# Centred output weights, the first batch's keys rotated on GpSimd, and new orders of work

## The chip, the cores and the metric

The kernel runs on one core of a Trainium2 chip. The metric is the device time of one launch in microseconds (us). Its engines are TensorE (PE: matrix products), VectorE (DVE), ScalarE (ACT), GpSimd (POOL) and SyncE (SP), whose queue issues the DMAs; each goes through its own instructions in order and waits on semaphores for the others. SBUF is the on-chip memory; PSUM holds the results of TensorE in eight banks.

## The reference, cut to what matters

```python
x = L0_attn_x                                        # (8, 1024, 256) fp32
x = x + layernorm(attn(layernorm(x)))                # 16 heads of 16, rotary, causal
x = x + layernorm(ffn(layernorm(x)))

def attn(x):                                         # qkv, bias, rotary on q and k
    scores = q @ k^T / 4, masked above the diagonal; softmax; @ v
    return out @ proj_w.T + proj_b
def ffn(x):
    return gelu(x @ U1 @ V1 + b1) @ U2 @ V2 + b2     # rank 64, 1024 wide
```

All is fp32. Both inner results go through a layernorm over the last axis (256) before they are added to the residual, so a mean over that axis that is taken out of the output weights and the output bias beforehand changes nothing in the end.

## The kernel before, in words

The work is eight batches of 1024 tokens; a batch has two halves `c` of 512 tokens, and four groups `g` of four heads. Per half: statistics and normalisation of the rows (`ln_*`), transposition (`xt`), products with the weights for queries and keys (`qk`; `p` is 0 for queries, 1 for keys) and values. Queries and keys are rotated (`rope`, three steps, function `rotate`, lines 537 to 553), rounded by ScalarE (`round`), and what the rounding left is computed (`rest`, function `rest_of`, line 555). Both parts are written to DRAM (`send`, line 624) and loaded back into QK in the layout that the scores need: for the first group in four pieces, one for each half and for keys or queries (`load_first`, line 634), for all others with `load_group` (line 649).

Per group TensorE computes all scores twice: `max` (twenty products, each reduced by VectorE, line 1015) for the rows' maxima, which are turned and written into QK as a further row (`shift`), and `score`, whose result ScalarE takes through the exponential (line 1206). GpSimd zeroes the part above the diagonal (`select`), and `product` multiplies with the values. A `max` over the second half of the sequence waits for both second-half pieces of the first load.

Behind the fourth group of a batch the heads' sums are inverted, `att_scale` multiplies, `proj` projects, and VectorE adds the bias (`proj_out`, line 1041). Then follows the layernorm of the result: statistics (`y_stats`, `y_dev`), GpSimd's `y_pow` (variance plus epsilon, minus the mean, power -0.5, their product), ScalarE's `y_rows` (line 1216: one instruction a row of tiles, scale and bias), and GpSimd's `residual` (line 1321). The feed-forward part runs behind the last groups over pieces `i` of 1024 tokens; its last layernorm is `f_spread`, `f_ypow`, `f_norm` (ScalarE, line 1245; two on VectorE in the last piece, line 1128) and `f_res` (GpSimd, line 1351; two on VectorE, line 1135).

The order of each engine's instructions is written out by hand as a string of letters, one for each step (`ORDERS`, line 154), and each of TensorE's results has its bank in a string of digits (`PLACES`, line 229). `taken_by` (line 126) says which engine has a step that could run on two. For batch 0 all of `rope` and `rest` is VectorE's, for the others GpSimd's:

```python
def rope_by(b, c, p):
    return "DVE" if b == 0 else "POOL"
```

Of the kernel before, what the change touches and what calls it, by code (L numbers as in the profile page):

```python
# [73 lines left out]
HALVES = (0, 1), (2, 3)  # L74


def steps_by_name():
# [4 lines left out]
        "ln_stats ln_rows y_stats y_rows": [(b, c, j) for b, c in halves for j in range(4)],  # L82
# [22 lines left out]
        "proj_out residual": [(b, c, q) for b, c in halves for q in (0, 2)],  # L105
        "first_turn first_turn_out first_low first_shift fold_weights fold fold_out f_load f_zero f_fill f_weights f_rest": [()],
# [8 lines left out]
        "f_norm f_res f_store": [(i, js, a) for i in parts for js in HALVES for a in (1, 0)],  # L115
# [5 lines left out]
def rope_by(b, c, p):  # L121

    return "DVE" if b == 0 else "POOL"


def taken_by(engine, step):

    what, *at = step
    if what in ("rope", "rest"):
        return engine == rope_by(*at[:3])  # L130
    if what in ("f_norm", "f_res"):
        last = at[0] == NB - 1 and at[2] == int(what == "f_norm")
        return (engine == "DVE") == last
    return True

# [20 lines left out]
        "HxxqqqqqqqqvvvvxxfqqqqqqqvqvvvxmmxmmmmqvFqqvhhmmqmmmqqmssqmssmqmsmsmvmvmsmxptmsmmsmxmssmpsmpmsssmsspssmsmq"  # L156
        "ssmqmssmmsspmsssmpmssmmsmmpsmmtpsssmssqqmssmpssmqmmssqsmpssmppsssmssqqssmmppmsssmsmsspssmsmpssmsspmsmtssmp"
        "mssmpssmspmssssspsssmpssmsssppmmssspssmspssmsspmssmspmssspmsssmpmssssptmsmsspmssmpmssmpsssmssmspssmspsmsms"
        "spmsssspmsmssppmsssmpssmsmspsmssmpssssmtpsssmmspssmsspmmssppmssvvmmssvvmssssxpsmssxsssmpppmmssqqmssmpssmqq"
        "mssmqqssssmvqvqvvssmmtpjmssmjpjssssmjmsssspmmsspxsssmspxppssssmqqqqmmsspqmssmqssmppsmssmqqssmmpjmssssjsmps"  # L160
# [131 lines left out]
def block_kernel(nc, x, w_qkv, b_qk, b_v, w_proj, b_proj, u1, v1, b1, u2, v2, b2,  # L292
# [27 lines left out]
    with ExitStack() as ctx:  # L320
# [425 lines left out]
        def tensor(e):  # L746
# [11 lines left out]
            for step in ORDER["PE"]:  # L758
# [649 lines left out]
```

## Time and profile before

| what | us |
|---|---|
| median of three runs (lowest, highest) | 1206.66 (1205.65, 1210.28) |
| the profiled execution, its time | 1208.03 |
| its span, first to last instruction | 1206.3 |
| TensorE busy | 1155.2 (96%) |
| VectorE busy | 941.1 (78%) |
| ScalarE busy | 941.8 (78%) |
| GpSimd busy | 658.8 (55%) |

The profile is of one execution. "PE" in it is a matrix product and "PEld" the load of its weights, which overlaps it; the ends of products are modelled, so products that follow closely count as busy throughout. Idle time stands with the engine and line that ended it. The granted clock (PEclk) is that of TensorE as a share of full speed.

### The profile page before, as it was taken

To read this page: it belongs to the slowest core of one execution; us is meant where nothing else is said; L and a number is where in the kernel's file an instruction comes from. 1 tells how busy PE (TensorE), PEld (TensorE's weight loads), DVE (VectorE), ACT (ScalarE), POOL (GpSimd) and SP (SyncE) were. 2 spreads that over 40 slices of the span, in tenths; PEclk is the share of its full clock that TensorE was granted. 3 is DMA by queue.
4 is the path that set the end of the run, shared out by engine and by line. 5 is a ranking of instruction groups with operands and counts; after the bars stand their busy time and mean duration, and the time that the engine had idled before them with its cause. 6 is when DMAs were issued, how large, how long until landed. Compare 5 with 4: busy or idle time off the path is not lost.

```text
span 1206.3 us, 25813 instructions
## 1 busy us (share of the span) xinstructions
PE 1155.2 (96%) x9844; PEld 619.4 (51%) x9844; DVE 941.1 (78%) x1458; ACT 941.8 (78%) x1898; POOL 658.8 (55%) x718
## 2 busy tenths in 40 slices
PE   5899999999999999999999999999999999999995
PEld 4655446544654456445654564455545554454542
DVE  6998786789678886888678958896888886476666
ACT  4477878788868877887878877887788689678785
POOL 2467325944495349633874387346844343336647
PEclk9899999999999999999999999999999999999998
DMA  6586544665555745576367636762766443402413
GB/s 202 180 143 127 106 66 79 159 130 103 111 140 132 133 81 142 128 107 140 93 147 104 144 81 152 115 151 37 177 117 127 100 96 114 131 1 92 154 54 122
DMA packets 99259, 142.22 MB, mean 118 GB/s; under 512 B 24896, under 2 KB 60992, under 8 KB 99136
## 3 DMA queue, kind: packets, MB, share of 16 engines
q1 hardware_dynamic: 99136, 140.58, 51.9%
q8 instruction: 78, 1.28, 0.5%
q14 instruction: 45, 0.37, 0.1%
HBM read 79.70 MB, written 51.38 MB: 109 GB/s over the span
## 4 chain that ended last, share of the span: by engine, by line
PE 63%; DMA 9%; SPq 8%; DVE 8%; POOL 7%; ACT 3%; issue 2%; DVEq 0%; POOLq 0%; ACTq 0%
PE PV L875 16%; PE RING L857 12%; PE RING L822 10%; PE RING L776 6%; DMA QK<-split_parts 4%; PE RING L886 3%; PE RING L789 3%; PE RING L927 3%; SPq L649 3%; PE RING L920 3%; SPq L624 2%; DVE MB L1015 2%; PE RING L828 2%; DMA X<-x 2%; ACT PB L1206 2%
## 5 line engine op out<-in xcount | busy, mean ns | idle before, releaser
L1206 ACT ACTIVATE PB<-RING 128x512 f32<-128x512 f32 (+2 forms) x1280 | 623.5, 566 | 139.4 <-PE RING L857 130.9
L1015 DVE TENSOR_REDUCE MB<-RING 128x2 f32<-128x1024 f32 (+2 forms) x448 | 497.0, 1142 | 96.1 <-PE RING L828 48.1
L857 PE MATMUL RING<-QK 64*128 64x512 f32 (+3 forms) x1536 | 320.5, 395 | 1.5 <-DMA QK<-NSROW 0.9
L1301 POOL TENSOR_SCALAR_AFFINE_SELECT PB<-PB 128x512 f32<-128x512 f32 x256 | 160.9, 638 | 275.1 <-ACT PB L1206 274.7
L822 PE MATMUL RING<-QK 62*128 62x512 f32 (+3 forms) x1536 | 296.2, 387 | 14.2 <-DMA QK<-split_parts 8.7
L857 PEld LDWEIGHTS RING<-QK 64*128 64x128 f32 x1536 | 169.2, 186 | 156.1 <-ACT PB L1206 92.3
L1015 DVE TENSOR_REDUCE M<-RING 128x2 f32<-128x768 f32 (+1 forms) x186 | 191.3, 1041 | 56.1 <-PE RING L828 55.3
L875 PE MATMUL PV<-PB,VL 128*32 128x512 f32 (+3 forms) x2048 | 224.1, 522 | 0.5
L822 PEld LDWEIGHTS RING<-QK 62*128 62x128 f32 x1536 | 156.7, 186 | 126.8 <-DVE MB L1015 36.3
L828 PE MATMUL RING<-MASKK,MASKQ 64*128 64x128 bf16 (+1 forms) x768 | 112.5, 248 | 0.0
L1231 ACT ACTIVATE F_H<-RING,F_B 128x512 f32<-128x512 f32 x128 | 80.5, 687 | 18.6 <-PE RING L920 18.5
L875 PE MATMUL PV<-PB,VU 128*32 128x512 f32 (+3 forms) x1024 | 89.4, 442 | 0.1
L546 POOL TENSOR_TENSOR TB<-EO,SIN 128x1024 f32<-128x1024 f32 x28 | 66.7, 2383 | 27.1 <-ACT EO L1167 22.9
L558 POOL TENSOR_TENSOR EO<-EO,PARTS 128x1024 f32<-128x1024 f32 x28 | 66.6, 2381 | 18.7 <-ACT PARTS L1172 18.7
L875 PEld LDWEIGHTS PV<-PB,VL 128*32 128x32 f32 x2048 | 44.9, 108 | 53.4 <-issue 32.8
L549 POOL TENSOR_TENSOR EO<-EO,COS 128x1024 f32<-128x1024 f32 x28 | 66.8, 2385 | 1.7
L1167 ACT ACTIVATE EO<-RING,BQS 128x512 f32<-128x512 f32 x60 | 41.3, 692 | 32.2 <-PE RING L776 29.6
L828 PEld LDWEIGHTS RING<-MASKK,MASKQ 64*128 64x128 bf16 x768 | 46.1, 94 | 39.0 <-issue 23.2
L886 PE MATMUL RING<-WP,ATT 128*32 128x256 f32 x1024 | 65.3, 382 | 0.1
L1306 POOL TENSOR_TENSOR ATT<-ATT,INV 128x512 f32<-128x512 f32 x32 | 40.8, 1285 | 36.7 <-DMA INV<-inverse_sums 36.6
L927 PE MATMUL RING<-F_H,F_U 128*64 128x512 f32 x256 | 60.0, 600 | 0.0
L776 PE MATMUL RING<-XTH,WQH 128*128 128x512 f32 x120 | 54.3, 453 | 2.6 <-DVE XTL L965 2.4
(141 smaller groups left out, 1507.8 us busy)
## 6 DMA issues: line engine op xcount, KB each, us to landing
QK<-split_parts SPq DMA_DIRECT2D x372, 128.0 KB, 5.8
split_parts<-PARTS SPq DMA_DIRECT2D x60, 256.0 KB, 3.1
split_parts<-EO SPq DMA_DIRECT2D x60, 256.0 KB, 3.6
ATT<-OT SPq DMA_DIRECT2D x128, 64.0 KB
INV<-inverse_sums SPq DMA_DIRECT2D x32, 256.0 KB
block_mid<-Y SPq DMA_DIRECT2D x16, 512.0 KB, 4.4
F_X<-block_mid SPq DMA_DIRECT2D x16, 512.0 KB, 5.6
out<-F_Y SPq DMA_DIRECT2D x32, 256.0 KB, 2.1
```

What stands on the lines that cost most here:

```text
L549: e.tensor_tensor(pair(b, c, p), pair(b, c, p), table(COS, c), ALU.mult).then_inc(r_t[by], 1)
L776: ins = e.matmul(bank, wq[:, k, 128 * m:128 * m + 128], xt[:, k, :], start=(k == 0 and n == 0), stop=(k == 1 and n == 2))
L822: ins = e.matmul(m[:, h, i, :], QK[g % 3][r, 0, k, 128 * t:128 * t + 128], QK[g % 3][r, 1, k, k0:k0 + n], start=(i == 0), stop=not open_en ...
L828: ins = e.matmul(m[:, h, :, n - 128:n], MASKQ[r, :], MASKK[r, :].unsqueeze(1).to_broadcast([64, len(pairs), 128]), start=False, stop=True)
L857: ins = e.matmul(m[:, i, :], QK[g % 3][r, 1, k, 128 * j:128 * j + 128], QK[g % 3][r, 0, k, 512 * c + off:512 * c + 512], start=True, stop= ...
L875: ins = e.matmul(PV[32 * h:32 * h + 32, off:512], v[:, n0:n0 + 32], PB[(SLOTS * g + s) % 4][:, h, 0:n], start=(j == 0), stop=(j == 4 * c + 3))
L886: ins = e.matmul(m[r:r + 32, :], ATT[c][:, k, 128 * q + r:128 * q + r + 32], WP[:, k, :], start=(k == 0), stop=(k == 1))
L927: ins = e.matmul(QP[64 * a:64 * a + 64, :], U2[:, f, :], H[i % 2][:, a, f, :], start=(f == 0), stop=(f == 7))
L1015: e.tensor_reduce(acc, ring(("max", g, s, u), pairs, n), AX.X, ALU.max).then_inc(v_max, 1)
L1206: e.activation(buf[:, h, pairs[0]:pairs[-1] + 1, :], strip(("score", g, s, u), pairs, n), ACT.Exp).then_inc(a_exp, 1)
L1231: e.activation(H[i % 2][:, a, f, :], GP[(NTH["up", i, f] - 1) % 2][a], ACT.Gelu_apprx_tanh, bias=B1[:, f:f + 1]).then_inc(f_g, 1)
L1301: e.affine_select(buf[:, :, 0:128], buf[:, :, 0:128], pattern=[[0, 4], [1, 128]], base=0, channel_multiplier=-1, compare_op=ALU.is_ge, fil ...
```

## The change

The output projection's weights and bias and the feed-forward part's last weights and bias are made to have mean zero over the 256 outputs, once, on VectorE (`centre`, `f_centre`). The projected rows then have mean zero, and the steps that carry the mean are gone: the shift in `y_pow` and `f_ypow`, and ScalarE's `y_rows` and `f_norm`. In their place GpSimd scales two rows of tiles at a time (`y_scale`), and `f_res` scales and adds: on GpSimd in two instructions for one half of the pieces, on VectorE in one instruction a row for the other half (`res_by`). In batch 0 the rotation of the second half's keys and the rests of both halves' keys go to GpSimd, and ScalarE's queue issues the first group's two loads of queries. All order strings and the bank string are new; TensorE has one step `warm` and one step `heat` more (products on zeros into a free bank).

The diff, cut to its core:

```diff
@@ rope_by, rest_by, taken_by, res_by @@
-    return "DVE" if b == 0 else "POOL"
+    return "DVE" if b == 0 and (c, p) != (1, 1) else "POOL"
+def rest_by(b, c, p):
+    return "DVE" if (b, p) == (0, 0) else "POOL"
+    if what == "load_first":
+        return engine == ("SP" if at[1] else "ACT")
+def res_by(i, js, a):
+    return "POOL" if (a == 0 if i < NB - 1 else (js, a) == (HALVES[0], 1)) else "DVE"
...
@@ ORDERS, PLACES: all strings new @@
...
@@ vector @@
+                elif what == "centre":
+                    w.wait_ge(o_mi["fold"], 1)
+                    e.tensor_reduce(MEAN[:, 0:2], WP[:, :, :], AX.X, ALU.add).then_inc(v_cen, 1)
+                    e.tensor_reduce(MEAN[:, 2:3], BP[:, :], AX.X, ALU.add).then_inc(v_cen, 1)
+                    w.wait_ge(v_cen, 2)
+                    e.tensor_scalar(MEAN[:, 0:3], MEAN[:, 0:3], -1.0 / D, None, ALU.mult).then_inc(v_cen, 1)
+                    w.wait_ge(v_cen, 3)
+                    for k in range(2):
+                        e.tensor_scalar(WP[:, k, :], WP[:, k, :], MEAN[:, k:k + 1], None, ALU.add).then_inc(v_cen, 1)
+                    e.tensor_scalar(BP[:, :], BP[:, :], MEAN[:, 2:3], None, ALU.add).then_inc(v_cen, 1)
+                elif what == "f_centre":
...
                 elif what == "proj_out":
-                    w.wait_ge(o_mi["fold"], 1)
+                    w.wait_ge(v_cen, 6)
...
                 elif what == "f_res":
-                    w.wait_ge(f_yna, NTH["f_norm", i, js, a])
-                    e.tensor_tensor(y[:, a, rows, :], y[:, a, rows, :], X1[i % 5][:, a, rows, :], ALU.add).then_inc(f_resv, 1)
+                    w.wait_ge(f_ypow, NTH["f_spread", i, js])
+                    for j in js:
+                        r = 4 * a + j
+                        ins = e.scalar_tensor_tensor(y[:, a, j, :], y[:, a, j, :], YF[i % 2][3][:, r:r + 1], X1[i % 5][:, a, j, :],
+                                                     ALU.mult, ALU.add)
+                    ins.then_inc(f_resv, 1)
@@ scalar @@
+                elif what == "load_first":
+                    load_first(e, w, *at)
-                elif what == "y_rows":
...
-                elif what == "f_norm":
...
@@ gpsimd @@
                 elif what == "y_pow":
-                    e.tensor_scalar(YNM[c][:, :], YMV[c][:, :, 0], -1.0, None, ALU.mult).then_inc(g_yve, 1)
-                    e.tensor_tensor(YNM[c][:, :], YNM[c][:, :], YRS[c][:, :], ALU.mult).then_inc(g_ynm, 1)
+                elif what == "y_scale":
+                    b, c, j0 = at
+                    w.wait_ge(g_yrs, NTH["y_dev", b, c])
+                    scale = YRS[c][:, j0:j0 + 2].unsqueeze(2).to_broadcast([128, 2, D])
+                    e.tensor_tensor(YS[c][:, j0:j0 + 2, :], YS[c][:, j0:j0 + 2, :], scale, ALU.mult).then_inc(g_ysc, 1)
                 elif what == "residual":
-                    w.wait_ge(a_yn, NTH["y_rows", b, c, 3])
+                    w.wait_ge(g_ysc, NTH["y_scale", b, c, j0])
...
                 elif what == "f_res":
+                    scale = YF[i % 2][3][:, 4 * a + js[0]:4 * a + js[-1] + 1].unsqueeze(2).to_broadcast([128, 2, D])
+                    e.tensor_tensor(y[:, a, rows, :], y[:, a, rows, :], scale, ALU.mult).then_inc(f_ysc, 1)
+                    w.wait_ge(f_ysc, NTH[step])
                     e.tensor_tensor(y[:, a, rows, :], y[:, a, rows, :], X1[i % 5][:, a, rows, :], ALU.add).then_inc(f_res, 1)
```

In ScalarE's order the first `load_first` stands ahead of the rounding of the second half's keys, the second behind `first_turn_out`. GpSimd's order begins `ln_pow(0,0) ones(1) ln_pow(0,1) rest(0,0,1) rope(0,1,1,0..2) ln_pow(1,0) rest(0,1,1)`. SyncE's is `load_x send(0,0,1) send(0,0,0) load_first(0,1) send(0,1,1) send(0,1,0) load_first(1,1) first_shift load_group(1)`. `centre` stands in VectorE's order in the third group. At the end VectorE has `f_res` for (7, (0,1), 0), (7, (2,3), 1) and (7, (2,3), 0), and GpSimd has `f_ypow(7, (0,1))`, `f_res(7, (0,1), 1)`, `f_ypow(7, (2,3))`.

## Rows read from the trace of the kernel before

**Rows 1.** The page, busy time, share of the span and instructions of each engine.

```profile
PE 1155.2 (96%) x9844; PEld 619.4 (51%) x9844; DVE 941.1 (78%) x1458; ACT 941.8 (78%) x1898; POOL 658.8 (55%) x718
```

**Rows 2.** Busy time by stretches; TensorE's clock, DMA share and GB/s come last.

```profile
core 0: us, PE busy (x) PEld busy (x) DVE busy (x) ACT busy (x) POOL busy (x), PEclk, DMA share, GB/s
43.40:56.00 12.60, 12.36 (x60) 8.78 (x60) 11.24 (x26) 3.96 (x8) 5.31 (x6) 0.59 0.70 221
56.00:72.00 16.00, 14.93 (x89) 8.52 (x88) 15.64 (x16) 8.50 (x17) 11.95 (x10) 1.00 0.76 116
72.00:96.00 24.00, 22.38 (x176) 11.92 (x176) 23.48 (x26) 16.92 (x33) 11.99 (x9) 1.00 0.52 108
96.00:1003.00 907.00, 894.90 (x8105) 477.64 (x8104) 731.62 (x931) 733.50 (x1517) 510.66 (x527) 1.00 0.57 118
...
1050.00:1191.00 141.00, 139.07 (x926) 71.31 (x924) 90.57 (x291) 113.94 (x205) 75.91 (x114) 1.00 0.26 87
1191.00:1206.30 15.30, 0.98 (x10) 0.53 (x6) 11.17 (x30) 4.04 (x8) 9.66 (x10) 0.70 0.39 137
```

**Rows 3.** Waits of TensorE, 100 to 1180 us: total, times, longest.

```profile
PE RING L822 <- DMA QK<-split_parts: 5.0, 6, 1.8
```

**Rows 4.** Order of time, VectorE, then ScalarE, 30 to 46 us: start, duration.

```profile
33.45 1.23 DVE L546 TENSOR_TENSOR Y<-PB,SIN 128x1024 f32<-128x1024 f32 x1 [0.28 <-ACT PB L1167]
...
36.58 0.68 DVE L553 TENSOR_TENSOR PB<-PB,Y 128x512 f32<-128x512 f32 x1
...
39.77 1.22 DVE L558 TENSOR_TENSOR PB<-PB 128x1024 f32<-128x1024 f32 x1
...
37.30 1.06 ACT L1172 ACTIVATE PB<-PB 128x1024 fp32r<-128x1024 f32 x1 [0.43 <-DVE PB L553]
```

**Rows 5.** Order of time, VectorE, 46 to 60 us; idle time before in brackets.

```profile
56.22 4.09 DVE L1015 TENSOR_REDUCE MB<-RING 128x2 f32<-128x768 f32 x4 [1.33 <-PE RING L828]
```

**Rows 6.** Order of time, SyncE's queue, 26 to 84 us.

```profile
35.78 5.85 SPq L634 DMA_DIRECT2D QK<-split_parts  x12
41.67 5.80 SPq L624 DMA_DIRECT2D split_parts<-PB  x8
47.52 6.13 SPq L634 DMA_DIRECT2D QK<-split_parts  x12
```

**Rows 7.** The chain that ended last: start, duration.

```profile
46.62 4.37 DMA split_parts<-PB
```

**Rows 8.** Order of time, GpSimd and VectorE beside each other.

```profile
31.66 0.23 POOL L1287 TENSOR_SCALAR VE<-MV 128x4 f32<-128x4 f32 x1 [11.89 <-DVE MV L977]
31.97 1.29 POOL L1288 TENSOR_SCALAR NM<-MV 128x4 f32<-128x4 f32 x1
...
31.95 1.22 DVE L558 TENSOR_TENSOR EO<-EO,PARTS 128x1024 f32<-128x1024 f32 x1
...
1106.39 1.27 POOL L1351 TENSOR_TENSOR F_Y<-F_Y,F_X 128x512 f32<-128x512 f32 x1
1106.45 1.68 DVE L1082 TENSOR_SCALAR F_XH<-F_X,F_MV,F_RS 128x256 f32<-128x256 f32 x2 [1.48 <-POOL F_RS L1329]
...
1080.94 1.38 DVE L1082 TENSOR_SCALAR F_XH<-F_X,F_MV,F_RS 128x256 f32<-128x256 f32 x4 [0.58 <-POOL F_RS L1329]
```

**Rows 9.** Groups of instructions: busy, mean ns; idle before, releaser.

```profile
L546 POOL TENSOR_TENSOR TB<-EO,SIN 128x1024 f32<-128x1024 f32 x28 | 66.7, 2383 | 27.1 <-ACT EO L1167 22.9
...
L1306 POOL TENSOR_TENSOR ATT<-ATT,INV 128x512 f32<-128x512 f32 x32 | 40.8, 1285 | 36.7 <-DMA INV<-inverse_sums 36.6
L1216 ACT ACTIVATE Y<-Y,YNM,YRS 128x256 f32<-128x256 f32 x64 | 37.6, 605 | 0.9 <-POOL YNM L1317 0.9
L552 POOL TENSOR_TENSOR EO<-EO,TB 128x512 f32<-128x512 f32 x26 | 33.5, 1287 | 1.5
```

**Rows 10.** Order of time, the last microseconds, GpSimd and VectorE.

```profile
1198.16 1.04 POOL L1343 TENSOR_TENSOR F_YRS<-F_YVE,HALF 128x4 f32<-128x4 f32 x1 [0.77 <-DVE F_YNM L1120]
...
1201.09 2.35 DVE L1135 TENSOR_TENSOR F_Y<-F_Y,F_X 128x512 f32<-128x512 f32 x2
```

More of the change, by code:

```diff
@@ L104, in steps_by_name @@
         "proj": [(b, c, q) for b, c in halves for q in range(4)],
-        "proj_out residual": [(b, c, q) for b, c in halves for q in (0, 2)],
-        "first_turn first_turn_out first_low first_shift fold_weights fold fold_out f_load f_zero f_fill f_weights f_rest": [()],
+        "proj_out y_scale residual": [(b, c, q) for b, c in halves for q in (0, 2)],
+        "first_turn first_turn_out first_low first_shift fold_weights fold fold_out centre f_centre f_load f_zero f_fill f_weights f_rest": [()],
         "f_stats f_pow f_rows": [(n,) for n in range(2 * NB)],
@@ L155 @@
     "PE": (
[L156 to L160, printed above, removed]
@@ L383, in block_kernel @@
             YRS = [sb(f"YRS{i}", [128, 4]) for i in range(2)]
-            YNM = [sb(f"YNM{i}", [128, 4]) for i in range(2)]
+            MEAN = sb("MEAN", [128, 4])
         def sb(name, shape, dt=fp32):
@@ L557, in rest_of, with load_first @@
             w.wait_ge(c_hi, NTH["round", b, c, p])
-            e.tensor_tensor(pair(b, c, p), pair(b, c, p), rounded(b, c, p).bitcast(fp32), ALU.subtract).then_inc(r_l[rope_by(b, c, p)], 1)
+            e.tensor_tensor(pair(b, c, p), pair(b, c, p), rounded(b, c, p).bitcast(fp32), ALU.subtract).then_inc(r_l[rest_by(b, c, p)], 1)
+        def load_first(e, w, c, p):
+            span = slice(512 * c, 512 * c + 512)
+            w.wait_ge(*parts_sent(0, c, p))
+            w.wait_ge(g_ones, 2)
+            for t, term in enumerate(TERMS_K if p else TERMS_Q):
+                src = split[0, term, p, 0:4, :, span].rearrange("(k h) f t -> h f k t", h=2)
+                for h in range(2):
+                    r0 = 64 * h + 16 * t
+                    e.dma_start(QK[0][r0:r0 + 16, p, :, span].bitcast(fp32), src[h]).then_inc(s_ld0 if c == 0 else s_ld[0], 16)
         def round_waits(w, b, c, p):
@@ L732, in sync @@
                     i, = at
-                    w.wait_ge(f_res, max(NTH["f_res", i - 5, js, a] for js in HALVES for a in range(2)))
+                    for a in range(2):
+                        w.wait_ge(f_resv if a else f_res, max(NTH["f_res", i - 5, js, a] for js in HALVES))
                     load_f(i)
@@ L736, in sync @@
                     i, js, a = at
-                    w.wait_ge(f_resv if i == NB - 1 and a == 0 else f_res, NTH["f_res", i, js, a])
+                    w.wait_ge(f_resv if res_by(i, js, a) == "DVE" else f_res, NTH["f_res", i, js, a])
                     rows = slice(js[0], js[-1] + 1)
```

276 lines of the change are left out of this document (130 added, 146 removed).

## The prediction

> **What bounds the kernel now.** I read the page's busy shares first: TensorE is busy 96% of the 1206.3 us span, VectorE and ScalarE 78%, GpSimd 55% [rows 1]. A share is an average, so the stretches came next [rows 2]. From 96 us (second group of heads done) to 1003 us TensorE is busy 894.9 of 907 us, and in the feed-forward stretch from 1050 to 1191 us 139.1 of 141. All that it waits for there in the open is 12.1 + 1.9 = 14.0 us; the largest named wait is for loads of QK, 5.0 us in six places [rows 3]. So for 1048 of 1206 us the kernel is bound by TensorE, and the change gives TensorE no less to do: the same 640 maxima, 1280 scores, 384 products, 128 + 64 + 64 projections. In the profiled run 1206.3 us of span lie in 1208.0 us of time; the sum below is made against that run, which stands 1.4 us above the median of 1206.7.
>
> Two pieces are bound by something else. Up to 96 us VectorE sets the pace: 11.2 of 12.6 us busy, then 15.6 of 16, then 23.5 of 24 [rows 2]. The gap inside it is the 1.33 us before 56.22, where VectorE waits for the first maximum over the second half of the sequence [rows 5]. That maximum, `("max", 0, 4, 0)`, needs both second-half loads of QK. After 1191 us TensorE has stopped (0.98 of 15.3 us) and VectorE (11.2) and GpSimd (9.7) finish the last batch.
>
> **The change, part by part.**
>
> *ScalarE.* It loses 64 row scalings of 0.605 us, 37.6 us in sum [rows 9], and those of the feed-forward part. They lie beside TensorE work, which is the bound. Floor: nothing. Ceiling: a share of the 14.0 us of open waits, since the exponential frees the PSUM banks sooner. I take 1.5 us of gain, with the new order of steps counted in it.
>
> *GpSimd, steady part.* It gains 32 `y_scale` of two rows each; the nearest row is the multiply of the same size, 1.285 us [rows 9], so 41 us, and loses the small shift instructions. At 55% that fits in, but each one stands ahead of a `select` or a rotation in its queue, and the product waits for the select. Between 0 (its idle time) and 1.3 us for each one that delays a product; I take 0.5 us in all.
>
> *Centring.* `centre` is six VectorE instructions over at most 512 elements a partition; a 512-element tensor_tensor took 0.68 us [rows 4], so at most 6 x 0.68 = 4.1 us and, the smaller ones by their elements, about 2.2 us. It stands inside group 2, after VectorE's saturated stage, where VectorE is busy 731.6 of 907 us. I take 0.2 us. `f_centre` is smaller and lies under TensorE: 0. The instructions that it lets go (mean times -1, shift times scale) are off the bound.
>
> *First batch: keys of the second half to GpSimd.* Before, VectorE started them at 33.45 and ended the rotation at 37.26; with the rest done between the queries' products, at 40.99 [rows 4]. SyncE's queue then sent keys and queries in eight issues from 41.67 to 47.47, the last landed 4.37 us after its issue, and the loads came behind [rows 6, 7]. GpSimd takes 2.38 for an instruction of 1024 elements and 1.29 for one of 512 [rows 9]: 2 x 2.38 + 2 x 1.29 = 7.3 us, then ScalarE's rounding 1.06 [rows 4], then the rest, 2.38. From 33.45 that is 44.3 at the earliest, 3.3 us later than now. The queue sends keys first, so both sends shift: four issues (0.61 each, without waits) bring 46.8, four more 49.3, against 47.5 now. That is 1.8 us later at the load and so at the first second-half maximum. ScalarE's queue takes the queries' loads: that saves SyncE six issues of 5.85/12 = 0.49 us in each half, 2.9 us [rows 6]. In the first half it helps the first maximum; in the second it takes back part, since the keys' six and the queries' six now run side by side, but the queries' load still waits until the last send has landed, and then takes its six issues. So it gives nothing on this path. If ScalarE's issues cost nothing it would give 2.9 us; if they cost what SyncE's do, they delay ScalarE's rounding of the keys behind them by up to 2.9 us. The two ends stay in the range.
>
> VectorE is relieved of 3.8 us of rotation and of two rests of 1.22, together 6.3 us. But this lies before 56.2, and what starts the saturated stage is the load. Relief before a wait turns into a longer wait.
>
> *Who else pays: the two engines block each other.* GpSimd's instruction on 128x4 elements takes 0.23 us at 31.66, but the next one, started at 31.97, takes 1.29, just as long as VectorE's two-input instruction of 31.95 runs [rows 8]. The other way round: four scalings take 1.38 us in sum at 1080.94, but the first two alone 1.68 at 1106.45, beside GpSimd's addition from 1106.39 to 1107.66. In the first batch the change puts GpSimd's 7.3 us of rotation and two rests of 2.38, 12.1 us, beside VectorE's remaining rotations and rests, all on two SBUF inputs. Per meeting the loser waits between 0 and 2.38 us. Some five instructions of VectorE meet GpSimd's. Floor 0, ceiling 5 us on the path to the last send. I take 2.2.
>
> [...]
>
> So the saturated stage begins 1.8 + 2.2 = 4.0 us later. The order on TensorE up to the end of group 1 holds the same steps but for two warming matmuls, so nothing else is done in that time and the shift goes through to 96 us and from there to the end.
>
> *The end.* Now: the last power ends at 1199.2, two small steps, a scaling and then the addition, to 1203.4, with the store behind it [rows 10]. After: `f_res` is one instruction a row, but `("f_res", 7, (0, 1), 1)` stands ahead of the last `f_ypow` in GpSimd's queue with two instructions of 1.29 us: the power starts about 1.6 us later. Behind it VectorE needs four instructions of 256 elements instead of 4.2 us; by 0.68 for 512 [rows 4] each is between 0.34 and 0.68, I estimate 0.42, so 1.7. 1.6 - 2.5 = -0.9 us; between -2.5 (no delay) and +1 (collisions as at 1201.09, where an addition of 0.6 took 1.2).
>
> Sum: +4.0 - 1.5 + 0.5 + 0.2 - 0.9 = +2.3 us. Against 1208.0: 1210.3; against the median: about 1209.
>
> **The rivals.**
>
> *A, faster.* The new order and the lighter ScalarE take away half of the 14.0 us of open waits (-7), and the keys do not come late, because VectorE is free to do the queries at once and ScalarE's loads start early (0 instead of +4); the end gives 0.9. That is 1206.7 - 8 = 1198.7. For it: ScalarE is busy 733.5 of 907 us in the steady part [rows 2], and each of its exponentials stands between a score and the bank that TensorE needs next. Against it: the named waits are for loads of QK and maxima, not for ScalarE.
>
> *B, slower.* GpSimd and VectorE shut each other out in full: +5 instead of +2.2 before the last send, and ScalarE's six issues ahead of the rounding add 1 to 2. The saturated stage begins 8 us late; with the rest as above 1206.7 + 8 - 1.7 = 1213. It decides if VectorE takes the first second-half maximum after 62 us instead of at 56.2. [...]
>
> *C, the moves in the first batch cancel.* The time of the last load stays within 1 us of now and only small terms are left: 1205.5. For it: GpSimd stands idle there, and an early start would hide its slowness.
>
> **How the numbers follow.** What a measurement of this kernel can tell from no change is about 0.5%, 6 us, so the borders are 1200.6 and 1212.7. The forecast has 0.38, A 0.22, B 0.20, C 0.20. The forecast's own range is 1204 to 1212. Faster gets A and a little of C, 0.24; slower B and the forecast's upper edge, 0.24; the same 0.52. The range that leaves two in ten out runs from 1198 to 1215.
>
> **What would show it.** Right: VectorE takes the first maximum over the second half near 60.2 us instead of 56.2, has a gap of some 5 us ahead of it and is full from there; GpSimd's rotation of PB lasts longer than 7.4 us or VectorE's two-input instructions beside it last longer than 1.23; the end of group 1 near 100; TensorE's open waits from there to the end of the feed-forward part of 10 to 15 us; the last power ahead of a shorter finish. Wrong: that maximum no later than 57, or open waits of TensorE under 8 us in the steady part (rival A), or over 20 (the queue of GpSimd would then be what I priced too low). The term that I know least is how the two engines share the first 60 us.

## The result, and the profile after

The changed kernel takes 1235.69 us (median of 3 runs, 1235.03 to 1237.04) against 1206.66 before: 1.0242 times as long, 95% interval 1.0208 to 1.0275. The forecast was about 1209, and 1215 was the upper end of its widest range. The profiled execution has a span of 1233.9 us, 27.6 more than before.

The page's busy shares, answering to [rows 1]:

```profile
PE 1164.0 (94%) x9846; PEld 622.4 (50%) x9846; DVE 968.1 (78%) x1489; ACT 886.0 (72%) x1774; POOL 690.0 (56%) x694
```

The stretches that answer to [rows 2], edges moved with the work, columns as there:

```profile
43.40:63.00 19.60, 11.64 (x64) 8.31 (x64) 13.96 (x25) 7.66 (x14) 8.91 (x10) 0.67 0.48 148
63.00:81.00 18.00, 17.44 (x89) 9.52 (x87) 15.50 (x17) 8.09 (x14) 12.60 (x7) 0.84 0.69 103
81.00:105.00 24.00, 23.16 (x178) 12.55 (x177) 23.97 (x28) 17.30 (x34) 11.43 (x13) 1.00 0.71 150
105.00:1023.00 918.00, 899.78 (x8106) 479.34 (x8104) 735.86 (x937) 710.10 (x1461) 533.18 (x527) 1.00 0.57 116
1070.00:1218.00 148.00, 139.89 (x918) 71.81 (x914) 110.20 (x317) 84.92 (x144) 73.52 (x86) 0.99 0.21 71
1218.00:1233.90 15.90, 1.92 (x16) 1.38 (x16) 11.88 (x30) 0.00 (x0) 9.87 (x9) 0.65 0.45 157
```

The loss is in three places, not one: the first batch (105 us instead of 96), the steady stretch (918 instead of 907 us) and the feed-forward (148 instead of 141). ScalarE has lost 56 us of work and TensorE gained nothing from it. TensorE is busy 8.8 us longer with the same matmuls but for two more on zeros: the time-weighted granted clock fell from 0.992 to 0.983.

A ledger says where. It compares one profiled execution with another, and takes the start of TensorE's `chain_turn(g)`, once a group, as the place that the kernel has reached, and of the last `f_y`; differences against before, in us:

```
                 group 0    1    2    3    9   15   21   26   31  last f_y  span
after               +9.1 +9.0 +13.7 +12.9 +11.8 +13.0 +14.6 +17.6 +20.1  +27.9 +27.6
```

So: first batch +9.1, group 2 +4.7, groups 3 to 31 +6.4, feed-forward +7.8, end -0.3.

**The first batch.** Order of time, 33 to 64 us, of GpSimd, VectorE, ScalarE (ACTq: its queue) and SyncE's queue in turn (start, duration; idle time before in brackets); it answers to [rows 4 to 6]:

```profile
33.58 2.39 POOL L561 TENSOR_TENSOR TB<-PB,SIN 128x1024 f32<-128x1024 f32 x1 [6.16 <-ACT PB L1201]
...
38.53 2.12 POOL L567 TENSOR_TENSOR PB<-PB,TB 128x512 f32<-128x512 f32 x1
40.62 2.24 POOL L568 TENSOR_TENSOR PB<-PB,TB 128x512 f32<-128x512 f32 x1
...
44.83 2.34 POOL L573 TENSOR_TENSOR PB<-PB 128x1024 f32<-128x1024 f32 x1
...
39.57 2.17 DVE L564 TENSOR_TENSOR PB<-PB,COS 128x1024 f32<-128x1024 f32 x1
...
44.98 0.38 DVE L998 BATCH_NORM_AGGREGATE MV<-ST 128x2 f32<-128x6 f32 x4 [2.58 <-POOL NM L1314]
45.28 2.44 DVE L567 TENSOR_TENSOR PB<-PB,Y 128x512 f32<-128x512 f32 x1
...
50.30 1.21 DVE L573 TENSOR_TENSOR PB<-PB 128x1024 f32<-128x1024 f32 x1
...
63.07 2.96 DVE L1036 TENSOR_REDUCE MB<-RING 128x2 f32<-128x768 f32 x3 [3.56 <-PE RING L847]
...
39.16 2.75 ACTq L584 DMA_DIRECT2D QK<-split_parts  x6
42.89 1.06 ACT L1208 ACTIVATE PB<-PB 128x1024 fp32r<-128x1024 f32 x1 [4.68 <-POOL PB L568]
...
57.40 2.85 ACTq L584 DMA_DIRECT2D QK<-split_parts  x6
...
47.19 6.80 SPq L650 DMA_DIRECT2D split_parts<-PB  x8
54.04 3.14 SPq L584 DMA_DIRECT2D QK<-split_parts  x6
```

GpSimd rotates from 33.58 to 42.86, 9.3 us in place of the 7.3 that its four instructions take alone; VectorE beside it needs 2.17 for 1.22 and, beside the rest, 2.44 for 0.68. The keys' rest, forecast to end at 44.3, ends at 47.17, and the sends wait for it. But the last four of the eight sends wait for the queries' rest on VectorE, which ends at 51.51 instead of 44.59; the wait of SyncE's queue for it, between two sends:

```profile
SPq L650 <- DVE PB L573: 1.9, 1, 1.9
```

The second queries' load starts on ScalarE at 57.40, 3.4 us after the last send, behind `first_turn_out`. VectorE's first second-half maximum is at 63.07, not 56.22 [rows 5]: 6.9 us late, where group 0's turned chain is 9.1 us late. The other 2.3 us are lost right behind that maximum, in TensorE's clock. TensorE waits 2.1 us for the loads of QK, up to 62.21, and then runs at its lower level:

```profile
62.20:68.80 6.60, 6.59 (x21) 3.94 (x21) 4.00 (x4) 0.92 (x2) 2.30 (x1) 0.50 0.76 114
```

VectorE, full at this place before [rows 2], is busy 4.0 of these 6.6 us.

**The centring and the feed-forward.** VectorE in group 2, order of time:

```profile
119.13 0.68 DVE L1054 TENSOR_REDUCE MEAN<-WP 128x2 f32<-128x512 f32 x1
...
120.86 1.31 DVE L1060 TENSOR_SCALAR WP<-WP,MEAN 128x256 f32<-128x256 f32 x2
122.09 2.45 DVE L1061 TENSOR_SCALAR BP<-BP,MEAN 128x256 f32<-128x256 f32 x1
```

The stretches around it:

```profile
110.00:120.00 10.00, 10.00 (x79) 5.40 (x76) 9.90 (x10) 8.05 (x18) 8.23 (x6) 1.00 0.92 125
120.00:130.00 10.00, 7.31 (x53) 3.13 (x51) 9.93 (x10) 5.72 (x12) 9.92 (x9) 0.85 0.41 72
```

TensorE's waits from 1023 to 1220 us (total, times, longest):

```profile
PE RING L919 <- DVE F_P L1133: 4.3, 2, 2.7
PE RING L919 <- DVE F_XH L1122: 2.7, 3, 1.5
```

The centring lasts from 119.13 to 124.54, 5.4 us; TensorE runs dry for 2.5 us, up to 125.72, and the clock of that stretch falls to 0.85. In the feed-forward TensorE waits 7.0 us for VectorE; before it was 1.2 there. Behind the longest of these waits, 2.7 us up to 1159.8, the clock is 0.50 from 1161.5 to 1164.5.

**The steady part behind group 2.** TensorE's wait for the loads of QK there, which was 5.0 us before [rows 3]; then the stretch from group 2's turned chain to group 31's, of the kernel before and of the changed one:

```profile
PE RING L841 <- DMA QK<-split_parts: 7.9, 6, 2.0
```

```profile
121.90:1003.10 881.20, 869.12 (x7895) 463.93 (x7893) 710.06 (x908) 712.66 (x1474) 491.24 (x513) 1.00 0.56 117
```

```profile
135.60:1023.20 887.60, 872.23 (x7892) 464.94 (x7892) 709.25 (x908) 688.68 (x1417) 512.14 (x511) 1.00 0.57 117
```

It is 6.4 us longer: TensorE is busy 3.1 us longer and idle 3.3 us longer, 2.9 of these for loads of QK.

### The profile page after: what moved, and what is told of

The parts are those of the page before. It is cut to its first block, busy times and chain, and to the rows that moved or that the text cites. A ratio compares the mean times of both kernels' runs of the same rounds, so it can differ in the third digit from the quotient of the medians.

```text
span 1233.9 us, 25681 instructions
## 1 busy us (share of the span) xinstructions
PE 1164.0 (94%) x9846; PEld 622.4 (50%) x9846; DVE 968.1 (78%) x1489; ACT 886.0 (72%) x1774; POOL 690.0 (56%) x694
## 4 chain that ended last, share of the span: by engine, by line
PE 53%; DVE 13%; POOL 12%; DMA 8%; SPq 7%; ACT 3%; issue 3%; ACTq 0%; POOLq 0%; DVEq 0%
PE PV L894 14%; PE RING L876 11%; PE RING L841 9%; PE RING L795 5%; DMA QK<-split_parts 4%; DVE MB L1036 4%; PE RING L906 3%; PE RING L940 3%; SPq L667 2%; POOL TB L561 2%; POOL EO L564 2%; PE RING L808 2%; PE RING L947 2%; SPq L650 2%; PE RING L847 2%
```

## The experiments

Medians are of 4 to 10 runs; "before" beside them had medians of 1205.4 to 1208.0. Most kernels take back or apply one part, with the letters of the order strings moved accordingly. Their ledgers first, in us against the kernel before:

```
              group 0     2     3     9    21    31  last f_y    median  ratio (95%)
after           +9.1 +13.7 +12.9 +11.8 +14.6 +20.1  +27.9    1235.7  1.0242 (1.0208-1.0275)
first_undone    -0.5  +1.6  +0.9  +0.0  +5.6 +10.8  +18.7    1224.2  1.0135 (1.0097-1.0172)
mid_undone      +8.1  +8.1  +8.2  +8.2  +5.3  +8.7  +29.5    1239.1  1.0255 (1.0236-1.0274)
ff_undone      +12.1 +19.5 +18.8 +20.1 +27.0 +30.3  +36.6    1237.7  1.0254 (1.0215-1.0293)
centre_gap      +9.8 +10.4  +9.7 +12.7 +15.7 +22.3  +30.2    1238.2  1.0244 (1.0212-1.0276)
keys_only       +9.0  +8.6  +8.7  +7.9  +5.1  +5.6   +5.3    1215.5  1.0071 (1.0051-1.0092)
loads_only      +4.7  +4.5  +4.5  +4.1  +5.1  +5.0   +6.3    1212.1  1.0047 (1.0024-1.0069)
scale_only      +0.6  +0.3  +0.3  +0.7  +0.0  +5.6   +8.0    1223.4  1.0123 (1.0091-1.0155)
scale_spread    +0.6  +0.2  +0.2  -1.3  -0.2  +1.7   +2.2    1206.8  1.0021 (1.0008-1.0034)
centre_only     +0.7  +1.2  +1.2  -0.1  -2.7  -0.8   -1.0    1205.6  1.0002 (0.9990-1.0014)
ff_only         +0.1  +0.6  +0.7  -0.6  -3.9  -3.4   -0.8    1209.3  1.0016 (0.9996-1.0036)
ff_orders       +0.1  -0.3  -0.3  -1.6  -1.2  -0.9   +3.2    1211.7  1.0038 (1.0021-1.0054)
probe2          +5.8  +5.5  +5.5  +6.1  +7.4  +8.5   +8.6    1211.9  1.0038 (1.0021-1.0055)
rot_dve         +8.8 +16.2 +15.4 +13.7 +17.5 +21.4  +30.6    1237.6  1.0255 (1.0237-1.0274)
loads_sp        +5.8 +13.4 +12.7 +11.7 +14.0 +20.0  +26.3    1235.6  1.0231 (1.0200-1.0263)
both_back       +4.0 +11.0 +10.3  +9.2 +15.2 +18.6  +26.3    1234.8  1.0214 (1.0179-1.0249)
dev_late        +7.4 +11.6 +10.9 +10.3 +15.3 +19.0  +26.6    1234.2  1.0227 (1.0182-1.0272)
```

A ledger is one execution, and executions differ. `ff_only` has before's steps up to group 31 and stands at -3.4 there; `ff_undone` has the changed kernel's and stands at +30.3, not +20.1. With before's orders the first columns repeat within about 1 us and the later ones within 4. With the changed first batch group 0 stood at 8.1, 9.1, 9.6 and 12.1 in four executions of the same steps: a difference of 1 or 2 us there says nothing. Nor is the profiled execution always a middle one: that of `probe2` was its slowest (1216.6 us), that of `ff_undone` too (1244.7), that of `scale_only` its fastest (1216.1).

Part of this spread is TensorE's granted clock. Between the first second-half maximum and group 0's turned chain 15.1 to 15.5 us pass in every kernel whose clock stays at 1.00 there, and 17.7 in the changed one. The maximum itself comes at 56.2 before and at 63.07 in the changed kernel; at 60.6 in `both_back`, 62.4 in `loads_sp`, 62.6 in `dev_late`, 63.0 in `rot_dve`, 55.8 in `first_undone`.

### Which region pays

**first_undone**: batch 0's rotations and rests on VectorE, all first loads on SyncE, every order up to group 0's turned chain as before.

```diff
-    return "DVE" if b == 0 and (c, p) != (1, 1) else "POOL"
+    return "DVE" if b == 0 and (c, p) not in () else "POOL"
...
-    return "DVE" if (b, p) == (0, 0) else "POOL"
+    return "DVE" if b == 0 and (c, p) not in () else "POOL"
...
-        return engine == ("SP" if at[1] else "ACT")
+        return engine == ("ACT" if tuple(at) in () else "SP")
```

> The changed kernel with its first batch taken back: all rotations and rests of batch 0 on VectorE, all first loads on SyncE's queue, and every engine's order up to group 0's turned chain as before the change; the rest as changed. Theory 1 (the price is paid where GpSimd's work stands beside VectorE's, separately in the first batch, at the centring, in the steady part and in the feed-forward): only the first batch's +9.1 us come back, 1226.5 (1225 to 1228). Rival (the later losses are consequences of the late first batch: the same work meets at worse times and with a lower granted clock): most of +29 comes back, 1212 or less.

Measured 1224.2 (1221.4 to 1229.1), 11.4 less. Theory 1's number was 9.1. Behind group 2 the losses stayed: from +1.6 there to +10.8 at group 31, and 7.9 in the feed-forward. They are no consequence of the late first batch. Group 2's loss did shrink, to 2.1 us from 4.6; the section on the centring shows why.

**mid_undone** and **ff_undone**: the steady part, or the feed-forward, as before in code and order (`y_rows` for `y_scale` and no `centre`; `f_norm` for half of `f_res` and no `f_centre`).

> The changed kernel with its steady part taken back: w_proj and b_proj not centred, ScalarE scales and shifts the projected rows (y_rows), and the orders between group 0's turned chain and the first f_turn as before the change; first batch and feed-forward as changed. Theory 1: the +4.7 us of group 2 and the +6 us of groups 22 to 31 go: 1225 (1223.5 to 1227). Rival (group 2's 4.7 us are the late first batch's and the steady part's 6 us are ScalarE's bands and the clock): 1231 to 1235.

> The changed kernel with its feed-forward taken back: no centring of v2 and b2, ScalarE scales and shifts the rows, GpSimd adds the residual, and the orders from the first f_turn on as before the change; the rest as changed. Theory 1 (scalar_tensor_tensor on VectorE and the broadcast scaling on GpSimd hold each other up): -8 us, 1228 (1226.5 to 1229.5). Rival (the feed-forward only ends late because its first half-group and its weights come late, or GpSimd is full): under -2 us, 1234 to 1236.

Measured 1239.1 and 1237.7: neither expectation. The ledger of `mid_undone` shows the steady part's 11 us gone (+8.1 at group 0, +8.7 at group 31), and then 20.8 us lost in the feed-forward. The longest wait of ScalarE there, and of VectorE in the feed-forward of `ff_undone`:

```profile
ACT Y L1253 <- POOL YNM L1345: 10.8, 1, 10.8
```

```profile
DVE F_ST L1107 <- DMA F_X<-block_mid: 6.2, 1, 6.2
```

These are seams of my own: ScalarE's `y_rows(7, ...)` stood where before's order has it, GpSimd's `y_pow(7, ...)` where the changed order has it; in `ff_undone` GpSimd's scaling of batch 7 stands ahead of the additions that free the buffer for the next load. So both totals prove nothing on their region; only the first one's ledger up to group 31 does.

### The first batch

**keys_only** and **loads_only**: one part each, in before's orders.

```diff
-    return "DVE" if b == 0 else "POOL"
+    return "DVE" if b == 0 and (c, p) not in ((1, 1),) else "POOL"
...
+    return "DVE" if b == 0 and (c, p) not in ((0, 1), (1, 1)) else "POOL"
```

```diff
+    if what == "load_first":
+        return engine == ("ACT" if tuple(at) in ((0, 0), (1, 0)) else "SP")
```

> The kernel before with one part of the change: GpSimd rotates the second half's keys and takes both halves' key rests, with its first eleven steps in the changed kernel's order; all other engines keep the order of before, with these steps taken out. Theory 1 (the part itself costs: GpSimd takes 9.3 us for the rotation, and it and VectorE hold each other up): +7 to +9 us, 1215. Rival (the part is cheap, the new orders around it cost): +3 us or less, 1207 to 1210.

> The kernel before with one part of the change: the queries' first loads of both halves start from ScalarE, after qk_out(0, 1, 1) and after first_turn_out, and not from SyncE. Theory (SyncE is spared 12 issues of 0.47 us, ScalarE pays 5.6 us in a stretch in which it waits for others): -1 to 0 us, 1206. Rival (ScalarE waits at the load for the sent parts, and round(0, 1, 1) behind it comes late): +2 us or more, 1209 or above.

Measured 1215.5 and 1212.1: either alone costs at once, +9.0 and +4.7 at group 0. Order of time: of `keys_only` GpSimd, ScalarE and VectorE, of `loads_only` ScalarE:

```profile
34.07 2.39 POOL L565 TENSOR_TENSOR TB<-PB,SIN 128x1024 f32<-128x1024 f32 x1 [6.15 <-ACT PB L1208]
...
40.24 1.26 POOL L572 TENSOR_TENSOR PB<-PB,TB 128x512 f32<-128x512 f32 x1
...
43.55 1.09 ACT L1193 ACTIVATE XH<-X,NM,RS 128x256 f32<-128x256 f32 x2 [8.20 <-POOL NM L1335]
44.55 0.67 ACT L1208 ACTIVATE PB<-RING,BQS 128x512 f32<-128x512 f32 x1
...
46.51 3.26 DVE L568 TENSOR_TENSOR PB<-PB,COS 128x1024 f32<-128x1024 f32 x1
```

```profile
38.39 2.78 ACTq L587 DMA_DIRECT2D QK<-split_parts  x6
41.22 1.06 ACT L1214 ACTIVATE PB<-PB 128x1024 fp32r<-128x1024 f32 x1 [4.85 <-issue]
```

Most of the price of `keys_only` came by another way than theory 1 said. The rotation took 7.4 us, without blocking, for VectorE stood idle: ScalarE's next normalised rows wait for a power that GpSimd does behind the rotation, and the last query band `qk_out(0, 1, 1)` stands behind them. Only the keys' rest, from 46.24 to 48.69 on GpSimd, then met VectorE's rotation: 3.26 us for 1.22, 2.0 us of blocking. In `loads_only` ScalarE waits for the sent parts and then issues; its rounding starts at 41.22 instead of 37.30 [rows 4], 3.9 us later.

**probe2**: nothing moved; GpSimd gets four instructions that nobody needs. (An earlier build, `probe`, never issued them and is a second copy of the kernel before: 1.0009, 0.9996 to 1.0023.)

```diff
+                elif what == "probe":
+                    for k in range(2):
+                        e.tensor_tensor(t, COS[:, :], SIN[:, :], ALU.mult).then_inc(g_probe, 1)
+                        w.wait_ge(g_probe, k + 1)
+                    e.tensor_tensor(TB[:, 0, :], COS[:, 0:512], SIN[:, 0:512], ALU.subtract).then_inc(g_probe, 1)
+                    e.tensor_tensor(TB[:, 1, :], COS[:, 512:1024], SIN[:, 512:1024], ALU.add).then_inc(g_probe, 1)
```

> The kernel before with an addition that nothing needs: from the end of ln_pow(1, 0) on, some 35 us, GpSimd runs four tensor_tensor instructions of the rotation's shapes (two of 128x1024, two of 128x512) on the tables and its own rotation buffer, 7.3 us by its rows, while VectorE rotates the second half's queries and takes the keys' rest (37.4 to 42.2). Theory 1 (the two shut each other out when both read SBUF, and that moves the end): VectorE's instructions there take up to 2.3 us in place of 1.23, group 0's turned chain comes 2 to 4 us later, 1208.5 to 1210.5. Rival (blocking shows in single rows but SyncE's queue or ScalarE covers it): no change, 1206 to 1207.

Measured 1211.9 beside 1208.0 of before, +5.8 at group 0. Order of time, VectorE, then GpSimd:

```profile
33.04 1.23 DVE L547 TENSOR_TENSOR Y<-PB,SIN 128x1024 f32<-128x1024 f32 x1 [0.27 <-ACT PB L1168]
34.30 3.46 DVE L550 TENSOR_TENSOR PB<-PB,COS 128x1024 f32<-128x1024 f32 x1
37.79 2.71 DVE L553 TENSOR_TENSOR PB<-PB,Y 128x512 f32<-128x512 f32 x1
40.43 1.75 DVE L554 TENSOR_TENSOR PB<-PB,Y 128x512 f32<-128x512 f32 x1
42.28 2.11 DVE L547 TENSOR_TENSOR Y<-PB,SIN 128x1024 f32<-128x1024 f32 x1
...
34.28 5.68 POOL L1290 TENSOR_TENSOR TB<-COS,SIN 128x1024 f32<-128x1024 f32 x2
40.04 1.59 POOL L1292 TENSOR_TENSOR TB<-COS,SIN 128x512 f32<-128x512 f32 x1
```

Four of VectorE's instructions take 10.0 us in place of 3.8, and the whole difference arrives at group 0. GpSimd's own step behind the probe, which fills a buffer for a later group, ends at 47.0, before the load that needs it, so the way goes over VectorE's late rotation: it ends at 42.2, not 37.3, and the sends start at 46.8, not 41.7. Blocking alone, in this place, costs group 0 more than the 2 to 4 us that the theory gave it; the median rose by 3.9 us.

**loads_sp**, **rot_dve**, **both_back**, **dev_late**: the changed kernel with the loads back on SyncE; the keys' rotation back on VectorE; both; or, last, only `rope(0, 1, 0, 2)` moved ahead of `ln_stats(1, 1, 2)`, `(1, 1, 3)` and `ln_dev(1, 1)`.

> The changed kernel with the queries' first loads back on SyncE's queue; GpSimd keeps the keys' rotation, orders as changed. Theory (in the changed kernel the load ends at 41.9 and ScalarE's round at 42.89 waits for GpSimd's rotation anyway, so the two parts cover each other): no change, 1235 to 1237, or up to 2 us more for SyncE's longer queue. Rival (the loads' 4.7 us are in the sum too): 1231.

> The changed kernel with the rotation of the second half's keys alone back on VectorE, ahead of the queries'; GpSimd keeps the key rests, ScalarE the queries' loads, orders as changed. Theory 1 (the rotation on GpSimd is what the first batch's 9 us come from): -7 us or more, 1228. Rival (ScalarE's wait for the sent parts ahead of round(0, 1, 1), 4.7 us when the loads moved alone, takes its place at once): -4 us or less, 1232 to 1235.

> The changed kernel with the keys' rotation back on VectorE and the queries' first loads back on SyncE, the key rests on GpSimd and the changed orders kept. Theory 1 (the two parts make the first batch's loss, each covered by the other when it is given back alone): 1227 (1225 to 1229). Rival (the changed orders of the first batch make it, with the parts: PE multiplies values before the last query bands and VectorE takes statistics ahead of the rotation): 1233 to 1237.

> The changed kernel with two statistics and ln_dev(1, 1) moved on VectorE from the middle of the queries' rotation to behind it (rope(0, 1, 0, 2) directly behind rope(0, 1, 0, 1)). Theory (VectorE's wait of 2.58 us for GpSimd's pow of ln_pow(1, 0), which stands behind the keys' rotation, is on the path): round(0, 1, 0) 3 us earlier, 1232.5 (1231 to 1234). Rival (the path goes over ScalarE's queue loads and SyncE's sends, or VectorE's instructions are held up by GpSimd's rotation instead): 1235 to 1237.

Group 0 stands at +5.8, +8.8, +4.0 and +7.4, for +9.1 (8.1 to 12.1). Part of these differences is the clock, so the first second-half maximum is the better mark. By it the loads given back yield only 0.7 us (62.4 for 63.07); the other 2.6 us at group 0 go with the clock behind it, 1.00 there and 0.50 in the changed kernel. The rotation given back alone yields nothing, since ScalarE's load takes its place (rounding at 43.08 instead of 42.89), as its rival said. Both given back yield 2.5 us; the other 4.8, to first_undone's 55.8, are the changed orders and the key rests on GpSimd. In `both_back` one of these rests meets VectorE:

```profile
40.69 3.40 DVE L564 TENSOR_TENSOR PB<-PB,COS 128x1024 f32<-128x1024 f32 x1
```

In `dev_late` VectorE ends the rotation 4.0 us earlier and the first second-half maximum comes only 0.5 us earlier: the sends start at 48.12, the second queries' load at 57.05. The eight sends now run in a row, up to 53.9, where the changed kernel's end at 54.0 with a pause in them: the keys' way over GpSimd and the queries' over VectorE are about equally long, and shortening one of them alone yields nothing.

The totals do not follow: 1235.6, 1237.6, 1234.8, 1234.2, all within 2 us of the changed kernel. What was won at group 0 was lost again in group 2 by the first and the third: group 2 costs +7.6, +7.4, +7.0 and +4.2, for +4.6 in the changed kernel. All four have the same 5.4 us of centring and the same wait of 2.5 to 2.6 us behind it. What differs is how long TensorE then stays at the lower level, here of `rot_dve` and of the changed kernel:

```profile
127.00:136.00 9.00, 9.00 (x58) 4.42 (x56) 5.31 (x7) 6.68 (x13) 4.85 (x4) 0.50 0.41 132
```

```profile
127.00:130.00 3.00, 3.00 (x19) 1.29 (x19) 3.00 (x3) 2.19 (x6) 2.92 (x3) 0.50 0.46 129
```

`loads_sp` and `both_back` have some ten microseconds at 0.50 too, `dev_late` three. Six or seven more at half speed lose about 3 us (an estimate), and group 2 differs by as much. Why the low stretch is longer in three of them stays open.

### The centring and GpSimd's scaling

**centre_gap**: the changed kernel, `centre` moved to VectorE's wait before `max_out(0, 4, 0)`. **centre_only**: the kernel before with `centre` where the change has it.

> The changed kernel with one step moved: VectorE centres w_proj and b_proj in its idle 3.6 us before max_out(0, 4, 0), where GpSimd has nothing to do, instead of in group 1 beside GpSimd's rotation. Theory 1 (the 5.4 us that the step took there held PE up by 2.5 us at once and cost 4.7 us by group 3's turn): 1231 (1230 to 1232.5). Rival (group 2's loss is the new order's or the clock's): no change, 1235.7 (1234.5 to 1237). Moving it could also delay the first bands: up to 1237.

> The kernel before with the centring of w_proj and b_proj alone, on VectorE behind max_out(2, 6, 1) as in the changed kernel; ScalarE scales and shifts as before. Theory (the step's price is 2.6 us of VectorE where GpSimd is idle and 5.4 us beside its rotation; only in the second case PE runs dry for 2.5 us and its clock falls): group 2 loses 1 us if the rows of the step show 2.6 us, 5 to 7 us if they show 5.4; 1208 or 1213. Rival (the centring is free, group 2's loss belongs to the changed order): under 1 us even with rows of 5.4.

In `centre_gap` group 2 cost 0.6 us, not 4.6, as theory 1 said; but a wait of 2.4 us ahead of group 9 took its place and the total is 1238.2 (1232.3 to 1240.7): the expectation of 1231 fell. `centre_only` is 1205.6, no change. The end of its step, beside which GpSimd is at a select or idle:

```profile
112.34 0.62 DVE L1061 TENSOR_SCALAR WP<-WP,MEAN 128x256 f32<-128x256 f32 x2
112.87 0.34 DVE L1062 TENSOR_SCALAR BP<-BP,MEAN 128x256 f32<-128x256 f32 x1
```

The last instruction takes 0.34 us here, 0.35 in `first_undone` and 2.45 in the changed kernel; there it starts at 122.09 and ends at 124.54, and GpSimd's first instruction of a rotation runs from 121.99 to 124.38. Alone the step takes 2.2 us, as forecast, beside the rotation 5.4, and only then TensorE runs dry: for 2.5 or 2.6 us in each of the seven traces with 5.4 us (the changed kernel, `ff_undone`, `after_yrows`, `rot_dve`, `loads_sp`, `both_back`, `dev_late`), for at most 0.3 us at once in `first_undone`, whose step takes 2.7 us.

**scale_only** and **scale_spread**: before's orders, feed-forward and first batch; `centre` in VectorE's gap; GpSimd scales, in the first each time right ahead of its residual, in the second two selects behind `y_pow`, one select apart.

> The kernel before with one part of the change: w_proj and b_proj are centred (in VectorE's wait before max_out(0, 4, 0)), and GpSimd scales the projected rows, each time just before it adds the residual, in place of ScalarE; orders and feed-forward as before. Theory 1 (GpSimd's 64 scalings of 1.05 us delay its selects and rotations and with them the steady part): +7 us, of which 1.5 at the centring, 1213.5. Rival (the steady part's 11 us are the new order's): +1 us, 1207 to 1208.5.

> As scale_only (1223.4: centring in VectorE's wait before max_out(0, 4, 0), GpSimd scales the projected rows, before's orders), but the scalings stand two selects behind y_pow and one select apart, not each right ahead of its residual; residuals where they were. Theory (scale_only's loss is that scaling and adding, 2.3 us in a row, stand in front of selects that PE's products wait for, 9.5 us in its trace): PE's waits for selects under 4 us, 1209 to 1212. Rival (GpSimd's added 64 us cost wherever they stand): 1218 or above.

Measured 1223.4 and 1206.8. TensorE's waits, 147 to 1009 us, of the first and the second:

```profile
PE PV L894 <- POOL PB L1337: 9.5, 10, 2.1
```

```profile
PE PV L894 <- POOL PB L1337: 0.8, 2, 0.6
```

What GpSimd is given, 32 scalings of 1.04 us, costs 16 us in one place of its queue and 1.4 us in another, centring included; 7 us more and a time of 1209 to 1212 were expected. (The profiled execution of `scale_only` was its fastest, 1216.1, with 8 of the 16 us; where the others lost the rest is not seen.) So neither the scaling nor the centring by itself makes the changed kernel's steady loss.

**after_yrows**: the changed kernel with ScalarE scaling again.

> The changed kernel with the projected rows scaled by ScalarE again (y_rows, some 10 to 28 bands after y_pow; eight groups of residuals some selects later on GpSimd, batch 7's among the feed-forward's gelus), all else as changed, the centring too. Theory 1 (GpSimd's scaling costs the steady part: in the trace of scale_only PE waited 9.5 us for selects, in the changed kernel 7.9 us for loads of QK): -6 to -10 us, 1228. Rival (the changed orders themselves cost it): 1234 to 1237.

Measured 1275.4 (1.0582, 1.0546 to 1.0619), a miss: my places for `y_rows` made TensorE wait 12.7 us for ScalarE and 10.8 for VectorE. Only between groups 9 and 22, where it ran quietly, does it say something: +5.8 us there without any scaling on GpSimd, as the changed kernel has (+4.8).

### The feed-forward

**ff_only**: the kernel before with `f_centre` and the split `f_res`, in before's orders. **ff_orders**: the same with the changed orders from the first `f_turn` on.

> The kernel before with one part of the change: v2 and b2 centred, VectorE scales and adds half of the feed-forward's rows (scalar_tensor_tensor, four steps after each f_spread), GpSimd the other half, ScalarE none; all other orders as before. Theory 1 (VectorE is too full for it: with it come F_P and F_XH late for PE): +6 to +8 us, 1214. Rival (the changed kernel's order of the feed-forward costs, not its split): +1 us or less, 1206 to 1208.

> The kernel before with the feed-forward's part of the change and the changed kernel's orders from the first f_turn on (ff_only had the part with before's orders, 1209.3); ScalarE still scales batch 7's projected rows, among the gelus at the places where the changed kernel's GpSimd does. Theory 1 (the changed order of the feed-forward costs its +7.8 us: f_rows and f_u1_out stand behind two f_res): 1216 (1214 to 1218). Rival (its loss comes from GpSimd's scaling of batch 7 and what waits behind that): 1209 to 1211.

Measured 1209.3, not told apart from before, and 1211.7. By the ratios they lose 1.9 and 4.6 us, with intervals that overlap; from group 31 to the last `f_y` 2.6 and 4.1 us, where the changed kernel loses 7.8. Groups of VectorE's instructions from the first `f_turn` on (busy, mean ns), of `ff_only`, then of the changed kernel:

```profile
L1123 DVE TENSOR_SCALAR F_XH<-F_X,F_MV,F_RS 128x256 f32<-128x256 f32 x64 | 25.0, 452 | 8.0 <-POOL F_RS L1362 8.0
L1168 DVE SCALAR_TENSOR_TENSOR F_Y<-F_Y,F_YRS,F_X 128x256 f32<-128x256 f32 x34 | 21.7, 682 | 0.6 <-POOL F_YRS L1375 0.5
```

```profile
L1122 DVE TENSOR_SCALAR F_XH<-F_X,F_MV,F_RS 128x256 f32<-128x256 f32 x64 | 30.6, 540 | 16.4 <-POOL F_RS L1353 16.3
L1167 DVE SCALAR_TENSOR_TENSOR F_Y<-F_Y,F_YRS,F_X 128x256 f32<-128x256 f32 x34 | 23.9, 745 | 3.9 <-POOL F_YRS L1366 3.9
```

So the part costs 2 to 3 us; that the orders bring more is not clear of noise. `f_rows` takes 452 ns in `ff_only`, 494 in `ff_orders` and 540 in the changed kernel (480 before); that it meets GpSimd oftener is my reading. In `ff_orders` TensorE waits 4.3 us for VectorE and its clock stays at 1.00; in the changed kernel it waits 7.0 and has the stretch at 0.50 behind the longest wait. These 3.7 us more go with the one piece that the changed feed-forward has and `ff_orders` lacks, batch 7's scaling on GpSimd; that is argued, not run alone.

## Why the prediction was wrong

**What bounds the kernel** was read rightly: TensorE, with two pieces that are not. But "bound by TensorE for 1048 of 1206 us" was taken for a shelter. It holds for work taken away; work added to VectorE or GpSimd broke it wherever it stood in front of something that TensorE waits for.

**The first batch, forecast +4.0, measured +9.1: this step failed first.** The forecast followed the keys alone: their rest at 44.3, eight sends in a row (1.8 us late), and 2.2 us for blocking. The keys' rest ended at 47.17: 2.0 us are the blocking of GpSimd's rotation, a term that was about right, and 0.9 are GpSimd's power, which stands between rotation and rest and outlasts the rounding. What set the last send was a path that the sum does not have, the queries' way over VectorE: its rotation was held up twice (2.17 us for 1.22, 2.44 for 0.68) and waited 2.58 us for that power, and the sends paused 1.9 us for the queries' rest. So the load started 6.5 us late (54.04 for 47.52), not 4.0. And 2.3 us of the 9.1 have no term in the sum either: TensorE's clock of 0.50 behind its wait for the late loads. Blocking can cost more than my ceiling of 5 in this place: probe2 shows 5.8 us at group 0 from blocking alone, in its slowest execution.

**"So it gives nothing on this path"**, of the loads on ScalarE: wrong by sign. They cost 4.7 us alone. Within the change they cost 0.7 us up to the first second-half maximum, by one execution each. I had the case in rival B as "1 to 2".

**"What starts the saturated stage is the load"** was right: VectorE's relief bought nothing, and it waited 3.56 us ahead of the first second-half maximum.

**The centring, forecast 0.2, measured 4.7.** Its duration of 2.2 us was right for VectorE alone. But it was priced by its elements and by VectorE's idle time, with no meeting with GpSimd, and it stood beside GpSimd's rotation: it took 5.4 us, TensorE waited 2.5 us, and the 3 us and more at 0.50 behind that lose another 1.5 at least. The warning stood in my own rows: the second example of blocking in [rows 8] is a tensor_scalar beside an addition on GpSimd. The Trainium skill ("SBUF — State Buffer", Who interferes with whom) counts tensor_scalar, copy and cast among those that can take the shared ports; the trace agrees (2.45 for 0.34 us).

**Steady part, forecast -1.5 + 0.5, measured +6.4 behind group 2.** ScalarE's 56 us brought nothing: TensorE did not wait for it before. GpSimd's scaling costs 1.4 or 16 us by its place, and its new orders place it well (TensorE waits 0.4 us for selects). I had said that open waits over 20 us would show GpSimd's queue priced too low; they came to 18.2 us in the steady stretch and 8.1 in the feed-forward, but not for GpSimd. What is left, 5 to 8 us, goes with the changed orders, as mid_undone's ledger and after_yrows' quiet stretch say, by one execution each; about half of it is waiting, above all for loads of QK (5.0 [rows 3] to 7.9 us). I found no single step that makes it. A wait can have a lower clock behind it, and need not: after the 1.9 us up to 914.4 the clock is 0.83 over ten microseconds, after the 2.0 us up to 660.8 it stays at 1.00.

**Feed-forward, no term but `f_centre`'s 0, measured +7.8.** The half of `f_res` that goes to VectorE was given no price ahead of the last piece. TensorE had no slack there against VectorE's `f_u1_out` and `f_rows`, and this half was put in front of them: TensorE's waits for VectorE rose by 5.8 us, and the clock behind the longest loses 1.5 more at least.

**The end, forecast -0.9, measured -0.3.** Right in both its parts, each a little off: the last power starts 9.0 us after the last `f_y`, not 6.6 (forecast 1.6 later), and 5.4 us before the end of the span, where it was 8.1 [rows 10] (forecast 2.5 less).

Rival B had the right mechanism and the right marker (the first second-half maximum after 62 us), and was priced for one region out of three.

No version beats the kernel before: `centre_only` and `ff_only` are not told apart from it, and every other part costs.

## What to carry over

Before work is moved to an idle engine, look at what stands behind it in that engine's queue, not at the share: the same scalings cost 16 us or 1.4. Where VectorE and GpSimd read SBUF side by side, price each meeting at up to the length of the other's instruction, tensor_scalar included (2.1 us more here, beside one of 2.39); probe it with instructions that nobody needs. A DMA issue on a compute engine waits for its data with the whole queue behind it (4.85 us in `loads_only`). Before two ledgers are compared, compare the granted clock of their stretches: the same wait of 2.5 us lost some 1.5 us behind it in one execution and 4.5 or more in another.

## What the runs showed of the hardware

A VectorE tensor_scalar of 256 elements takes 0.34 us alone and 2.45 beside a GpSimd tensor_tensor; two of them take 0.62 alone and 1.31 beside GpSimd's selects; VectorE's two-input ones of 1024 elements go from 1.23 to 3.46, GpSimd's from 2.38 to 2.84 (5.68 for two). GpSimd's scaling by a broadcast column took 1.04 us for 512 elements where the addition of the same shape took 1.26; forecast was 1.285. TensorE's granted clock was 1.00 until its wait of 2.5 us, which ended at 125.72, and 0.50, the lower of its levels of 2.4 and 1.2 GHz, from 127 to 130; in `rot_dve` the same wait has 0.50 from 127 to 136 behind it: the wait is paid twice.
